# A decoder layer on one core: moved input turns, rotary work on VectorE at the start, the bias added ahead, and the experts' order

## The reference

```python
x = _layernorm(x + _L0_attn_ref(x, Wqkv, bqkv, Wo, bo))            # 16 heads of 16, rotary, causal
x = _layernorm(x + _L0_xattn_ref(x, mask, ctx, Wq, Wk, Wv, Wo, gate))  # 32 heads of 8: causal, plus gated adapter keys and values from ctx
x = _layernorm(x + _L0_ffn_ref(x, ...))
# _L0_ffn_ref: a = attention(layernorm(h)), 16 heads of 128, rotary, with output bias bo
#              h = h + a;  m = moe(layernorm(h));  return h + m
# moe: raw = softmax(x @ w_gate); the top 2 of 4 experts get softmax weights (comb);
#      hmid = gelu(x @ we1 + be1); out = sum over e of comb[e] * (hmid[e] @ we2[e] + be2[e])
```

## Time and profile before

| | us |
|---|---|
| median of 3 runs | 1250.82 (1248.06 to 1252.48) |
| the profiled execution | 1250.7 |
| its span, first to last instruction | 1248.9 |
| PE busy in the span | 1150.0 (92%) |
| DVE busy | 980.1 (78%) |
| ACT busy | 656.4 (53%) |
| POOL busy | 667.1 (53%) |
| mean granted clock of PE | 0.979 of full |

### The profile page before, as it was taken

The page is one execution under the profiler, slowest core; times in us unless marked ns, Lnnn a source line. Parts: engine busy times, 40 slices in busy tenths (PEclk is TensorE's granted clock), DMA queues, the critical chain, the costliest instruction groups (busy, mean ns, idle before and its releaser), DMA issues.

```text
span 1248.9 us, 29536 instructions
## 1 busy us (share of the span) xinstructions
PE 1150.0 (92%) x11172; PEld 941.1 (75%) x11172; DVE 980.1 (78%) x2259; ACT 656.4 (53%) x1685; POOL 667.1 (53%) x715
## 2 busy tenths in 40 slices
PE   4799899899999999878999999999999999998998
PEld 4576676566676666545899889988999888887886
DVE  2667686788889888977888788878888788957877
ACT  3455564375766766564555534444444444456563
POOL 6666574444545455253778554445444454346555
PEclk9899899899999999989999999999999999999999
DMA  8664443333333333301221000000000100001110
GB/s 214 164 155 116 107 116 87 82 93 98 103 101 105 84 107 94 112 19 56 81 68 53 1 1 2 1 2 1 1 2 1 34 2 18 18 3 34 34 37 32
DMA packets 98286, 76.22 MB, mean 61 GB/s; under 512 B 73531, under 2 KB 86459, under 8 KB 98145
## 3 DMA queue, kind: packets, MB, share of 16 engines
q1 hardware_dynamic: 98145, 74.34, 22.0%
HBM read 53.40 MB, written 19.92 MB: 59 GB/s over the span
## 4 chain that ended last, share of the span: by engine, by line
PE 58%; DVE 20%; issue 8%; POOL 8%; ACT 5%; DMA 0%; DVEq 0%; POOLq 0%; SPq 0%; ACTq 0%
PE bank L1413 4%; PE bank L512 4%; PE bank L1414 4%; PE bank L1415 4%; PE bank L1469 4%; PE bank L1442 4%; DVE B_nr L637 4%; DVE PT L646 3%; PE bank L448 3%; PE bank L375 3%; PE bank L455 3%; PE bank L490 2%; PE bank L1429 2%; PE bank L1431 2%; PE bank L1430 2%
## 5 line engine op out<-in xcount | busy, mean ns | idle before, releaser
L1710 POOL TENSOR_TENSOR C_QK<-C_t1b,C_t2b 128x512 f32<-128x512 f32 x128 | 166.9, 1304 | 247.2 <-DVE C_t2b L1554 247.0
L1551 DVE SCALAR_TENSOR_TENSOR C_t1b<-bank,C_bcol,C_tabs 64x512 f32<-64x512 f32 x256 | 192.0, 750 | 53.5 <-PE bank L1415 49.3
L637 DVE TENSOR_REDUCE B_nr<-bank 128x4 f32<-128x512 f32 x256 | 164.4, 684 | 37.5 <-PE bank L455 36.3
L1413 PE MATMUL bank<-C_XTh,C_Wh 128*128 128x512 f32 x256 | 112.8, 440 | 5.4 <-POOL C_XTl L1402 3.8
L863 ACT ACTIVATE PT<-bank 128x512 f32<-128x512 f32 x160 | 91.8, 596 | 48.8 <-PE bank L490 48.5
L1662 ACT ACTIVATE C_V<-bank 128x512 f32<-128x512 f32 x64 | 38.1, 597 | 147.7 <-PE bank L1431 146.1
L858 ACT ACTIVATE PT<-PT 128x512 f32<-128x512 f32 x96 | 59.5, 631 | 93.5 <-DVE PT L646 93.5
L1643 ACT ACTIVATE C_P<-bank,C_nm 128x128 f32<-128x128 f32 x256 | 90.5, 367 | 31.8 <-DVE C_nm L1564 30.2
L1414 PE MATMUL bank<-C_XTl,C_Wh 128*128 128x512 f32 x256 | 101.9, 398 | 0.0
L1415 PE MATMUL bank<-C_XTh,C_Wl 128*128 128x512 f32 x256 | 101.1, 395 | 0.0
L512 PE MATMUL bank<-PT,vpool 128*32 128x128 f32 x2048 | 97.4, 286 | 3.5 <-ACT PT L858 3.4
(11 more groups left out here) (254 smaller groups left out, 3713.4 us busy)
## 6 DMA issues: line engine op xcount, KB each, us to landing
Adrq<-PB SPq DMA_DIRECT2D x16, 192.0 KB, 2.8
stk<-Adrq SPq DMA_DIRECT2D x16, 192.0 KB
Adrk<-PB SPq DMA_DIRECT2D x16, 192.0 KB, 2.8
stk<-Adrk SPq DMA_DIRECT2D x16, 192.0 KB
Bdrq<-PB SPq DMA_DIRECT2D x16, 192.0 KB, 2.9
stk<-Bdrq SPq DMA_DIRECT2D x32, 96.0 KB
Bdrk<-PB SPq DMA_DIRECT2D x16, 192.0 KB, 2.7
stk<-Bdrk SPq DMA_DIRECT2D x32, 96.0 KB
```

The source lines that it names most:

```text
L637: e.tensor_reduce(dst, bank[n % 2][:, :].rearrange("p (a b) -> p a b", a=4), AX.X, ALU.max, negate=True).then_inc(sem("m_dve"), 1)
L1413: e.matmul(o[:, :], CWh[hp][:, cs], XCh[0][:, t, :], start=t == 0, stop=False)
L1551: e.scalar_tensor_tensor(out=v4(t1b[kq][lo:lo + 64, :]), in0=v4(o[hi:hi + 64, :]), scalar=bc[hi:hi + 64, :], in1=tabsC[hi:hi + 64, 2 * kq ...
L1710: e.tensor_tensor(QK[v % 3][:, kq, :], t1b[kq][:, :], t2b[kq][:, :], ALU.add).then_inc(sem("rc_pool"), 1)
```

## The change

It has five places.

1. **Start (chunks 0 and 1).** The first weight load is split in two, and the weights' high and low parts are made in four pieces of 256 columns: the low parts of the pieces for q and k by DVE, the others by POOL (`weights_low`). The k projection comes one step after q's instead of four. Of chunks 0 and 1, the rotary products, the sum and the roundings of q0, k0 and k1 are done by DVE instead of POOL (`FIRST`), k's with buffers of their own (`rope_buffers`). The stacked layouts are read per batch, q and k in turn.
2. **A.** x of the chunks 1 to 7 is transposed one step sooner (chunk 2: two), in the step of the k projection of the chunk before; ACT's copy waits for that projection. Batch 15's turn and output product come later (steps 81 to 84 and 83 to 87).
3. **A to B.** Chunk 8's two inputs are transposed in steps 40 and 42 instead of 44 and 45. The clearings of the value pool are moved: the first two from step 44 to 28 and 32, the last from 82 to 88, one of two from 55 to 59.
4. **C.** POOL adds the output bias to X in advance, one batch at a time in units 8 to 11 of a chunk (12 to 15 in the first), instead of four batches after the residual. The fourth hidden product of the first experts' chunk stands ahead of the last output product but one.
5. **D.** The next chunk's input is turned at m = 5 and 6 instead of 4 and 5. The combination weights are transposed after the second hidden product instead of the first, and the constant part (b2) goes to the second expert's bank. POOL's residual is made per batch, and its rstd for the norm stands ahead of the one for the output.

The diff, cut to its core:

```diff
-    xts = places((-1,), (1, 0), (-2, 2), (-8, 8))
+    xts = places((-1,), (-2, -4), (-2, 2), (-8, 8))
     projs = places((2, 6), (2, 6, 10), (0, 8, 13), (-5, 10, 13))
+    for c_ in range(2):
+        del projs[bg0(c_) + 6]
+        projs[bg0(c_) + 3] = (c_, 1)
+    for c_ in range(1, 8):
+        del xts[bg0(c_) - 1]
+        xts[bg0(c_) - (3 if c_ == 2 else 2)] = (c_, 0)
...
+    for s_ in [k for k, v in stacked.items() if v[0][0] < 2]:
+        del stacked[s_]
+    for c_ in range(2):
+        stacked[bg0(c_) + 12] = [(c_, 0, 0), (c_, 1, 0), (c_, 0, 1), (c_, 1, 1)]
...
     def wo_step(g):
-        return to_step(g, 1) + (4 if g < 16 else 8 if g < 31 else 5)
+        return to_step(g, 1) + (4 if g < 14 else 4 if g < 15 else 8 if g < 16 else 8 if g < 31 else 5)
...
-    backs = {wo_step(g) - (3 if 16 <= g < 31 else 2): g for g in range(32)}
+    backs = {wo_step(g) - (2 if g == 14 else 3 if g == 15 else 3 if 16 <= g < 31 else 2): g for g in range(32)}
...
+    def rope_buffers(c, ti):
+        if c < 2 and ti == 1:
+            return [T[:, :].rearrange("p (f s) -> p f s", f=2) for T in (PT[0], PT[2], PT[1], OTf)]
+        return ab, tt[:, 0:2, :], tt[:, 2:4, :], y
+
+    BY_DVE = (0, 1, 3)
+    FIRST = [divmod(k, 2) for k in BY_DVE]
...
     def dve_ab(e, steps):
...
-            split_weights(0, (0,))
         for s in steps:
             if s == 2 - AHEAD:
-                split_weights(0, (1,))
+                split_weights(0, 0)
+                split_weights(0, 1)
...
+            if ropes.get(s) in FIRST:
+                rope(e, q, *ropes[s])
+                rope_sum(e, q, *ropes[s])
+            for part in range(2):
+                if splits[part].get(s) in FIRST:
+                    split(e, q, *splits[part][s], part)
...
         def x_high(c, n):
             q.wait_ge("xt_pe", v_xt(c, n))
             if c > 8 or (c and not n):
                 if c < 8:
                     q.wait_ge("v_pe", 2 * c)
+                    q.wait_ge("pj_pe", k_proj(c - 1, 1) + 1)
                 elif c == 8:
                     q.wait_ge("v_pe", 16)
+                    q.wait_ge("pj_pe", k_proj(7, 1) + 1)
...
+    INITS = {28: (0, 0), 32: (0, 1), 55: (1, 0), 59: (1, 1), 63: (2, 0), 71: (2, 1), 79: (3, 0), 88: (3, 1)}
+
     def pool_ab(e, steps):
...
         for s in steps:
-            if s == 44:
-                init_values(0, 0)
-                init_values(0, 1)
...
+            if s == 3 - AHEAD:
+                weights_low(2)
+            if s == 4 - AHEAD:
+                weights_low(3)
+            if s in INITS:
+                init_values(*INITS[s])
...
             load(ident[:, :], I["c_ident"], "ld_c")
             load_x(0)
-            load_weights(0, 0)
+            load_weights(0, 0, "ld_wA0", slice(0, 256))
+            load_weights(0, 0, "ld_wA1", slice(256, 512))
...
     def pe_c(e):
...
+        hidden_pe(e, q, 0, 3)
         out_proj(NU - 2)
-        hidden_pe(e, q, 0, 3)
...
     def dve_c(e):
...
-                q.wait_ge("saved", 256)
+                q.wait_ge("xb_c_pool", bi + 1)
                 e.tensor_tensor(X[:, bi, :], bank[4 + b // 2][:, (b % 2) * 256:(b % 2) * 256 + 256], X[:, bi, :],
                                 ALU.add).then_inc(sem("xc_dve"), 1)
...
     def pool_c(e):
...
-        def residual(c):
+        def add_bias(bi):
             q.wait_ge("ld_boC", 16)
-            for b in range(4):
-                bi = 4 * c + b
-                q.wait_ge("xc_dve", bi + 1)
-                e.tensor_tensor(X[:, bi, :], X[:, bi, :], boC[:, :], ALU.add).then_inc(sem("xc_pool"), 1)
+            q.wait_ge("saved", 256)
+            if bi >= 4:
+                q.wait_ge("xn_dve", 4 * (bi // 4))
+            e.tensor_tensor(X[:, bi, :], X[:, bi, :], boC[:, :], ALU.add).then_inc(sem("xb_c_pool"), 1)
...
-            if u >= 2 and (u - 2) % 16 == 15:
-                residual((u - 2) // 16)
             soft(u)
...
+            if 0 <= r - (8 if c else 12) < 4:
+                add_bias(4 * c + r - (8 if c else 12))
...
-        residual(NCH - 1)
...
+    XT_FIRST = 5
...
+    CONSTANT = [1] * (NCH - 1) + [2]
...
     def pe_d(e):
...
-                if c + 1 < NCH and 4 <= m < 6:
-                    xt_pe(e, q, c + 5, m - 4, dturn_bank(q, ("xt", c + 5, m - 4)))
+                if c + 1 < NCH and XT_FIRST <= m < XT_FIRST + 2:
+                    xt_pe(e, q, c + 5, m - XT_FIRST, dturn_bank(q, ("xt", c + 5, m - XT_FIRST)))
                 hidden_pe(e, q, c, m)
                 if m == 1:
+                    comb_t_pe(e, q, c - 1)
                     gate_pe(e, q, c)
-                if m == 0:
-                    comb_t_pe(e, q, c - 1)
...
     def pool_d(e):
...
-        def residuals(c):
+        def residual(c, b):
             q.wait_ge(f"ld_x2{c % 2}", 16 * (c // 2 + 1))
-            q.wait_ge("xc_pool", 4 * c + 4)
-            e.tensor_tensor(X2[c % 2][:, :, :], X2[c % 2][:, :, :], X[:, 4 * c:4 * c + 4, :], ALU.add).then_inc(sem("x2_pool"), 4)
+            q.wait_ge("xc_dve", 4 * c + b + 1)
+            e.tensor_tensor(X2[c % 2][:, b, :], X2[c % 2][:, b, :], X[:, 4 * c + b, :], ALU.add).then_inc(sem("x2_pool"), 1)
...
-                if m == 5:
-                    residuals(c)
+                if m < 3:
+                    residual(c - 1, m + 1)
+                if m == 7 and c + 1 < NCH:
+                    residual(c, 0)
+                if m in LAST and c + 1 == NCH:
+                    residual(c, LAST.index(m))
```

262 lines of the change are left out of this document (146 added, 116 removed).

## The result

The changed kernel takes 1232.09 us (median of 4 runs, 1230.73 to 1233.84) beside 1251.65 us for the kernel before (4 runs, 1248.06 to 1253.67). The ratio is 0.9848, 95% interval 0.9821 to 0.9874, so it is 1.5% faster. In a second comparison the same code came to 0.9838 (0.9825 to 0.9852). The forecast was 1225.5 with a range of 1214 to 1237: sign and range held, but of the 25.3 us 5.7 did not come in the medians (19.6 measured), and 6.8 in the spans of the two profiles (18.5). Most of this part is about those.

The account below looks back on a forecast made before the run. The prediction took PE (TensorE), busy 1150.0 of 1248.9 us, to bound the kernel. Its seven terms summed to 25.3 us, taken off 1250.8 for 1225.5 us, with a range of 1214 to 1237.

Parts of the forecast that it names:

- What bounds the kernel: Whole kernel: PE sets the pace, busy 1150.0 of 1248.9 us; time to win is its 99 us idle and lower-clock stretches.
- 1. Start: Before the first attention unit: rotary chains on DVE, k sooner and split weights start it at 29 to 31 us; minus 6.5 us.
- 2. A's turns: Input turns in the self-attention: one step more of lead removes two PE waits for x's low part; minus 2.0 us.
- 3. Chunk 8: Chunk 8's input turns, moved earlier: PE's 3.73 us wait and the lower clock behind it go; minus 5.0 us.
- 4. Batch 15: Steps 80 to 90: later turn and output product remove PE's 2.00 us wait behind DVE's division; minus 2.5 us.
- 5. Bias: Layer's attention: output bias added ahead in pieces removes PE's waits at three chunk ends, pieces costing nothing; minus 4.2 us.
- 6. Last chunk: Last chunk of attention: an expert product put ahead covers PE's wait for an output's low part; minus 1.1 us.
- 7. Experts: Experts: later weights' transpose, bias gone and residual in pieces shorten PE's waits, lower clock not counted; minus 4.0 us.
- The sign on the 16-column operation: Experts: DVE's 16-column weight product, 2.26 us beside POOL's residual, would take under 0.8 us in the changed profile.
- Little start: Rival: DVE collisions or loads holding q0's and k0's parts leave the start 0 to 2 us; taken 1232, chance 0.17.
- Slower: Rival: ACT's copy of x waits for the k projection, delaying exponentials and PE in seven chunks; 1258 us, chance 0.06.
- The clock goes too: Rival: half-clock stretches at chunk 8, steps 80 to 90 and experts vanish whole, start gives 8; taken 1216, chance 0.12.

## Why the prediction was right, and what it got wrong

**What bounds the kernel** held: PE is as busy as before, and the whole gain is waits (PE's listed waits add up to 66 us from 60 us on before, and to 55 now; the start gave 5 to 6 more) and half clock (some 52 us of the span before, 37 and 33 in the two profiles of the changed kernel, each us worth half of one).

**1. Start**, forecast -6.5, measured -4.9 and -5.9. First projection 7.22 (forecast 7.0), q0's and k0's parts out at 19.52 and 20.53 (17.5 and 18.7), first unit 32.2 to 32.9 (29 to 31). The size was about right and the attribution wrong, so that this term came out is luck. The step that failed is the gain given to DVE's rotary work, with the loads' backlog weighed only as the bound. The runs show that DVE's 4.3 us become 0.9 at the first read and nothing that can be told at unit 16, and the split load's 0.9 us become none; what PE waits for at the first unit is a transfer, whoever computed the parts. A part of the start, 0.5 to 2.9 us at unit 16, is the earlier turn of x, which I had booked under A. The rest wasn't taken apart; likely it is k one step behind q, since with the rotary work on GpSimd in both, k0's parts are written at 24.94 instead of 29.86 before.

**2. A's turns**, forecast -2.0, measured +0.4 in A (and -0.5 to -2.9 in the start). The step that failed is "one step more of lead is longer than the wait", with up to 0.2 us of new wait: I followed the turn in its queue, and not the bank that it takes from the rotation. The next user of that bank waited 0.58 us, three times, and the output's low part came 0.39 late twice. The sign that I had named, no wait over 0.5 us at the turns of chunks 4 and 5, failed with it.

**3. Chunk 8**, forecast -5.0, measured -2.3 by undoing it alone. "Next late would be the projection's own bank, some tenths" is the failed step: next late were x's own turn, 1.30 us, and the output's turn behind it, 0.58, for the same reason. The clock's part was there, but 3.4 us of half clock instead of the 6.8 in the earlier trace rows in the undone kernel.

**4. Batch 15**, forecast -2.5 with up to -5.4, measured -3.0 in the landmarks and -3.4 to -4.1 by undoing it. The mechanism held, a part of the clock's share with it.

**5. Bias**, forecast -4.2 and no less than -3.6, measured -0.5 to -1.7. The three waits went as said, 3.7 us. "The pieces cost nothing" is the failed step: POOL was idle enough, but I took an average (53% busy, and one idle row) for cover at every place. One piece was put in front of the operation on which PE waits next, and three beside DVE where DVE was full.

**6. Last chunk**, forecast -1.1: from the last landmark of the units to the first C_XN turn -1.3. Held.

**7. Experts**, forecast -4.0, measured -5.7. PE's waits in this stretch fell from 6.5 us to 2.2, 4.3 us where the sum had 4.0: the term held. The rest fits the clock, which I had left out: three stretches of 3.4 us at half clock before (from 1139, 1173 and 1204 us), one of 6.8 in the changed kernel, 1.7 us in all. With other profiles of the same code the term would be -5.0 to -8.2. The sign on the 16-column operation, under 0.8 us, failed: it took 1.15 us, not beside a piece of the residual, which I had taken for the longest that can hold it, but beside a low part of 128x512. It didn't matter, since PE doesn't wait for it there.

**The rivals.** "Little start" fits the mechanism (the parts are held by transfers, whoever computes them) and was wrong about the price: 4.9 to 5.9 us came all the same, in part by the turns of x. "Slower" didn't come: no wait of ACT for the k projection shows behind exponentials. "The clock goes too" came in part: PE's mean granted clock rose from 0.979 to 0.985.

In all, in the order of the table, -25.3 became -18.5 and -19.6 in the two profiles: +0.6 to +1.6 at the start, +4.1 in A and chunk 8, -0.5 at batch 15, +1.2 or -0.3 of clock between 234 and 644 us, +2.4 to +3.2 in the layer's attention, -1.7 in the experts. That the total lies near the forecast is in part luck: the terms that fell short by 4.1 and by up to 3.2 us stand against two that gave 1.7 and 0.5 more.

## What to carry to other kernels

When an operation is moved to an earlier place, three queues have to be looked through, not one: the engine's, the buffer's that it takes (here a bank in rotation, whose next user inherits the wait), and that of whoever must copy it out. An engine that is half idle on average isn't free at each place: for each moved piece read what stands right behind it there, and whether someone waits for that. Work that ends in a transfer is worth speeding up only if the transfer can start; read the time from write to read beside the loads that run then (5.8 us for parts written at 19.5, 2.4 for those written at 23.8), before moving arithmetic to a faster engine. Here the next thing to try would be to issue the adapter's loads later; it wasn't tried.
